# Attention over images on one core: the first query step beside the last key tiles, and the next pair's first convolution early among the queries

## What is computed

```python
x = x + conv_block(group_norm(x))      # 1x3, 5x5 and 1x5 convolutions, a correlation over 7 shifts
t = to_tokens(x)
t = t + attention(layer_norm(t))       # the change lies here
t = t + experts(layer_norm(t))         # top-8 tokens for each of 32 experts

def attention(x):                      # 16 heads of 64
    q = elu(x @ wq.T + bq) + 1;  k = elu(x @ wk.T + bk) + 1;  v = x @ wv.T + bv
    kv_cos, kv_sin = sum_s (k*cos) v,  sum_s (k*sin) v          # 64 x 64 for each head
    o = (q*cos) @ kv_cos + (q*sin) @ kv_sin
    denom = 1 / ((q*cos) @ sum_s(k*cos) + (q*sin) @ sum_s(k*sin) + 1e-5)
    return (o * denom) @ dense_w.T + dense_b
```

## Time and profile before

| | |
|---|---|
| time, median of 3 runs | 3526.32 us (3520.82 to 3526.87) |
| the profiled execution's own time | 3529.31 us |
| its span, first to last instruction | 3527.5 us |
| mean granted clock of TensorE | 0.982 of full speed |
| PE busy | 3191.5 us, 90% of the span |
| DVE busy | 2415.9 us, 68% |
| ACT busy | 1975.6 us, 56% |
| POOL busy | 1968.3 us, 56% |

### The profile page before, as it was taken

One profiled execution on the slowest core, in us unless ns is written; L12 is line 12 of the kernel. 1 busy time (PEld: TensorE's weight loads), 2 busy tenths in 40 slices (PEclk: granted clock), 3 DMA queues, 4 the chain that ended last, 5 costly groups with the idle time before them and its releaser, 6 DMA issues.

```text
span 3527.5 us, 44913 instructions
## 1 busy us (share of the span) xinstructions
PE 3191.5 (90%) x17092; PEld 1488.6 (42%) x17092; DVE 2415.9 (68%) x2773; ACT 1975.6 (56%) x2209; POOL 1968.3 (56%) x1303
## 2 busy tenths in 40 slices
PE   3898999989899998989989898998989999899977
PEld 2543345434443335433454344443354333543333
DVE  5887766967668676776668666686756866645754
ACT  1166654766556764666646665476645676444430
POOL 1167861878428882478727785297833888121320
PEclk8999999999999999999999999999999999999988
DMA  2002740046300661016510363005620075202678
GB/s 55 19 1 57 156 104 28 1 98 146 82 19 0 145 143 56 1 29 152 133 31 0 80 152 85 28 1 125 141 60 19 2 161 135 52 1 65 149 169 279
DMA packets 69297, 278.75 MB, mean 79 GB/s; under 512 B 30845, under 2 KB 35485, under 8 KB 64221
## 3 DMA queue, kind: packets, MB, share of 16 engines
q1 hardware_dynamic: 69085, 275.89, 32.5%
HBM read 242.78 MB, written 33.05 MB: 78 GB/s over the span
## 4 chain that ended last, share of the span: by engine, by line
PE 72%; DVE 11%; ACT 7%; DMA 5%; issue 4%; SPq 1%; POOL 0%; DVEq 0%; ACTq 0%; POOLq 0%
PE ps_D L1590 15%; PE ps_C L1523 10%; PE ps_A L1508 5%; PE ps_B L1508 5%; PE ps_D L1523 5%; PE ps_E L1568 5%; PE ps_E L1523 5%; PE ps_B L1552 3%; PE ps_D L1366 3%; PE ps_A L1552 3%; DVE region L1149 2%; PE ps_A L1385 2%; DMA RB<-r_keep 2%; DVE arena L1000 2%; DMA r_keep<-RR 2%
## 5 line engine op out<-in xcount | busy, mean ns | idle before, releaser
L610 POOL TENSOR_TENSOR arena<-arena,UHL 128x896 f32<-128x896 f32 x525 | 1106.6, 2112 | 252.8 <-ACT UHL L771 252.6
L1590 PE MATMUL ps_D<-region,small 128*128 128x448 f32 x1792 | 759.3, 550 | 9.7 <-DVE OS L1185 6.6
L592 POOL TENSOR_TENSOR region<-region,RB 128x896 f32<-128x896 f32 x224 | 468.9, 2093 | 174.9 <-DMA RB<-r_keep 174.5
L771 ACT ACTIVATE UHL<-arena,W8C 128x896 f32<-128x896 f32 x525 | 540.9, 1033 | 0.4
L620 POOL TENSOR_TENSOR UA<-region,CS 128x128 f32<-128x128 f32 (+1 forms) x400 | 224.6, 563 | 449.4 <-PE ps_C L1523 401.3
L1590 PEld LDWEIGHTS ps_D<-region,small 128*128 128x128 f32 x1792 | 322.9, 190 | 291.8 <-issue 237.8
L815 ACT ACTIVATE EQ<-ps_B,NEG 128x896 f32<-128x896 f32 x224 | 225.5, 1007 | 361.4 <-PE ps_B L1552 361.4
L1523 PE MATMUL ps_C<-region,UA 128*128 128x512 f32 (+1 forms) x800 | 382.5, 601 | 18.1 <-ACT region L689 18.1
L1000 DVE SCALAR_TENSOR_TENSOR arena<-arena,W8C 128x448 f32<-128x448 f32 (+1 forms) x235 | 358.3, 1545 | 0.0
L1158 DVE TENSOR_TENSOR region<-region,ps_C 128x896 f32<-128x896 f32 x224 | 242.9, 1084 | 142.3 <-ACT ps_C L779 142.0
L1125 DVE SCALAR_TENSOR_TENSOR region<-region,ps_A 128x1024 f32<-128x1024 f32 (+1 forms) x200 | 242.6, 1213 | 140.2 <-ACT region L797 140.2
(11 more groups left out here) (308 smaller groups left out, 4983.8 us busy)
## 6 DMA issues: line engine op xcount, KB each, us to landing
RB<-r_keep SPq DMA_DIRECT2D x448, 448.0 KB, 6.0
arena<-x SPq DMA_DIRECT2D x8, 1568.0 KB, 6.6
t_keep<-Y SPq DMA_DIRECT2D x7, 1568.0 KB, 5.2
r_keep<-RR SPq DMA_DIRECT2D x448, 7.0 KB, 2.9
w_keep<-region SPq DMA_DIRECT2D x7, 784.0 KB, 5.5
arena<-w_keep SPq DMA_DIRECT2D x4, 784.0 KB, 10.6
arena<-L_ffn_weight SPq DMA_DIRECT2D x1, 2080.0 KB
CST<-cst SPq DMA_DIRECT2D x1, 1568.0 KB, 6.4
```

The source lines that it names most:

```text
L592: pool.tensor_tensor(out=q, in0=q, in1=RB[:, cc].rearrange("p (c n) -> p c n", c=2), op=ALU.mult).then_inc(pool_scaled.sem, 1)
L610: pool.tensor_tensor(out=X[:, cut], in0=X[:, cut], in1=PRODUCT[m % 3], op=ALU.add).then_inc(pool_taps.sem, 1)
L771: act.activation(PRODUCT[m % 3].rearrange("p (h w) -> p h w", w=W), g_window(2 * g * ROWS + 2 * (k // 5), 2 * (k % 5) - 4, 2 * ROWS), ACT. ...
L1590: ins = pe.matmul(here.area(key)[:, 0:PIX], MW[i][:, c, :], Q[s % 3][:, c, :], start=c == 0, stop=c == NCHUNK - 1)
```

## The change

Three things move, and no work is removed or added.

1. Step 0 of the queries (first image) moves into the key tiles of the second image: the two head matrices of the first image go behind `k_project` of tiles 29 and 31, the four `q_project` of step 0 behind that of tiles 33, 35, 37 and 39, the denominators to tile 41, the sums and the reciprocal to tile 43. All of these use ps_C, one after the other. DVE's part stands one tile later, and in the eight tiles 30, 32, 34, 36, 38, 40, 42 and 43 DVE does no depthwise piece; six pieces go to tiles 44 to 49, two to slots 12 and 15. Step 0's features lie in buffers that are free at that time, and its chunks 0 and 2 are scaled by DVE out of SBUF (`first_scale`), without ACT's copy to PSUM.
2. The slots begin with step 1 and are 66 in place of 70. The head matrices of the second image stand in slots 1 and 3, the four outputs of step 0 in slots 2, 4, 6 and 8. `q_project(1, 0)` goes ahead of the last `k_products`.
3. The four parts of `front` go from slots 57, 59, 61 and 63, in ps_A and ps_B, to slots 4, 6, 8 and 10, in ps_C. The slots of the tap products become a little denser, four in five slots in place of three in four.

The diff, cut to its core: the constants, the uses of the PSUM areas, then DVE's function and PE's.

```diff
-K_PIECES, FRONT_PIECES, Q_PIECES, DRAIN_PIECES = 1, PIECES, (1, 0, 0, 1), 1
-PRODUCT_TILE, PRODUCT_SLOT, POOL_LAG, DRAIN_SLOT = 20, 3, 4, 64
+FRONT_PIECES, Q_PIECES, DRAIN_PIECES = PIECES, (1, 0, 0, 1), 1
+HEAD_TILES, FIRST_TILES, FIRST_DEN, FIRST_SUM = (29, 31), (33, 35, 37, 39), 41, 43
+NO_PIECE = (30, 32, 34, 36, 38, 40, 42, 43)
+PRODUCT_TILE, PRODUCT_SLOT, POOL_LAG, PIECE_SLOT, DRAIN_SLOT = 20, 1, 1, 12, 60
-PRODUCT_SLOTS = {PRODUCT_SLOT + n + n // 3: n for n in range(POOL_PIECES - TILE_PRODUCTS)}
-SLOTS = 4 * STEPS
+PRODUCT_SLOTS = {PRODUCT_SLOT + n + n // 4: n for n in range(POOL_PIECES - TILE_PRODUCTS)}
+SLOTS = 4 * (STEPS - 1)
+HEAD_SLOTS = (1, 3)
+FIRST_OUT_SLOTS = {2: 0, 4: 1, 6: 2, 8: 3}
+FIRST_POOL_SLOTS, FIRST_PARTS_SLOT = {0: 1, 2: 3}, 10
-FRONT_SLOTS = {SLOTS + s: g for g, s in enumerate((1, 3, 5, 7))}
-ALL_SLOTS = 70
+FRONT_SLOTS = {4: 0, 6: 1, 8: 2, 10: 3}
+ALL_SLOTS = 66
...
-            uses += [(("m", i, g), misc()) for i in range(2) for g in range(2)]
+                uses += [(("m", 0, HEAD_TILES.index(k)), "C")] if k in HEAD_TILES else []
+                uses += [(("qp", 0, FIRST_TILES.index(k)), "C")] if k in FIRST_TILES else []
+                uses += [(("den", 0), "C")] if k == FIRST_DEN else []
+                uses += [(("dsum", 0), "C")] if k == FIRST_SUM else []
...
-                uses += [(("t2", FRONT_SLOTS[j]), "AB"[FRONT_SLOTS[j] % 2])] if j in FRONT_SLOTS and not last else []
+                uses += [(("t2", FRONT_SLOTS[j]), "C")] if j in FRONT_SLOTS and not last else []
...
+            def first_scale(here, cc):
+
+                q = features(0, cc)
+                dve.wait_ge(*spread_loaded[cc // 2].at(here.pair, 1))
+                dve.tensor_tensor(out=q, in0=q, in1=RB[:, cc].rearrange("p (c n) -> p c n", c=2),
+                                  op=ALU.mult).then_inc(first_scaled.sem, 1)
...
+                    if k - 1 in HEAD_TILES:
+                        head_matrices(here, 0, HEAD_TILES.index(k - 1))
+                    if k - 1 in FIRST_TILES:
+                        q_features(here, 0, FIRST_TILES.index(k - 1))
+                    if k == FIRST_DEN + 1:
+                        den_parts(here, 0)
+                    if k == FIRST_SUM:
+                        den_guard(here, 0)
+                        den_reciprocal(here, 0)
+                    if conv and k > NORM_TILE and k not in NO_PIECE:
+                        depthwise(here, pair + 1, 1, DVE_PIECES)
+                first_scale(here, 0)
...
+                    if k in HEAD_TILES:
+                        head_matrices(here, 0, HEAD_TILES.index(k))
+                    if k in FIRST_TILES:
+                        q_project(here, 0, FIRST_TILES.index(k))
+                    if k == FIRST_SUM:
+                        q_sums(here, 0)
+                    if k == KTILES + 1:
+                        q_project(here, 1, 0)
...
+                    if j in HEAD_SLOTS:
+                        head_matrices(here, 1, HEAD_SLOTS.index(j))
...
+                    if j in FIRST_OUT_SLOTS:
+                        q_output(here, 0, FIRST_OUT_SLOTS[j])
```

More of the change, by code:

```diff
@@ L95, in slot_of_step, with step_of, chunk_of @@
 def slot_of_step(j, lag):
[L96 removed]
+    return j >= lag and (j - lag) % 4 == 0 and (j - lag) // 4 < STEPS - 1
+def step_of(j):
+    return j // 4 + 1
+def chunk_of(j):
+    return j // 4 + 1, j % 4
 def copied_slot(j):
@@ L676, in tokens @@
                     act.wait_ge(*square_free)
+                if which == 2 and g == 0:
+                    act.wait_ge(*here.filled(("out", 0)))
                 src = here.area(key)[:, 0:m * P].rearrange("p (t c) -> p t c", c=P)
@@ L789, in products_out, with q_exponential @@
                         .then_inc(*here.empty(key))
+            def q_exponential(here, s, cc):
+                key = ("qp", s, cc)
+                act.wait_ge(*here.filled(key))
+                act.activation(EQ[:, cc % 2], here.area(key)[:, :].rearrange("p (c n) -> p c n", c=2)[:, :, 0:PIX],
+                               ACT.Exp, bias=NEG1[:, 0:1]).then_inc(eq_ready.sem, 1)
             def pair_of_images(here):
@@ L808, in pair_of_images @@
                         products_out(here, 0)
-                products_out(here, 1)
                 for j in range(ALL_SLOTS):
                     if j < SLOTS:
[L813 to L817, removed]
+                        q_exponential(here, *chunk_of(j))
+                    if j == 0:
+                        products_out(here, 1)
                     if here.span == "loop" and j in PRODUCT_SLOTS:
@@ L1145, in q_features @@
                 dve.wait_ge(*eq_ready.at(here.pair, n + 1))
-                if s >= 3:
+                if s == 1 and cc == 0:
+                    dve.wait_ge(*ua_ready.at(here.pair, KTILES))
+                if s >= 4:
                     dve.wait_ge(*(here.filled(("out", s - 3)) if cc == 3
@@ L1587, in q_output @@
                 pe.wait_ge(*(scaled_by_pool(here.pair, s, cc) if cc in POOL_SCALED
-                             else here.emptied(("rb", s, cc))))
+                             else here.emptied(("rb", s, cc)) if s else first_scaled.at(here.pair, cc // 2 + 1)))
                 for c in (2 * cc, 2 * cc + 1):
-                    ins = pe.matmul(here.area(key)[:, 0:PIX], MW[i][:, c, :], Q[s % 3][:, c, :],
+                    ins = pe.matmul(here.area(key)[:, 0:PIX], MW[i][:, c, :], features(s, cc)[:, c % 2, :],
                                     start=c == 0, stop=c == NCHUNK - 1)
@@ L1618, in pair_of_images @@
                         k_products(here, k - 2)
+                    if k == FIRST_DEN:
+                        for g in range(2):
+                            q_denominators(here, 0, g)
                     if k in UTS_TILES:
```

139 lines of the change are left out of this document (77 added, 62 removed).

## The result

The changed kernel takes 3603.97 us (median of 4 runs, 3601.97 to 3607.94) against 3526.6 for the kernel before: a ratio of 1.0219, with a 95% interval from 1.0197 to 1.0241. It is 77 us slower. The sign was forecast, the size was not: 3549 was predicted, with 3571 as the upper end.

The account below looks back on a forecast made before the run. PE was taken as the fullest engine, so its idle time was summed: 3.7 - 2.4 + 0.5 + 1.2 = +3.0 us a loop pair, +21 for seven, +1.3 for the last; together +22 on 3526.3, 3549 us (range 3518 to 3571).

Parts of the forecast that it names:

- Key tiles: Key tiles: 7.15 us of added waits for ps_C less 3.4 us given back by the pieces, net +3.7 a pair.
- Start and steady steps: Start of queries: idle 8.7 against 11.1 us, -2.4; steady steps: two pieces in DVE's queue beside POOL, +0.5 a pair.
- front(0): Start of queries: front's first part waits 1.8 us for ps_C from the copy of head (1,1).
- front(3): Start of queries: front's last part, sharing ps_C with the spread of step 1, waits 2.6 us (0.3 to 3.0).
- the denominators: Start of queries: step 1's denominators wait 2.0 us behind first_scale(2), POOL and a copy.
- a piece until 4.3, POOL's turn until 6.4: Start, counted in us from the end of k_project(49): DVE's piece, then one POOL instruction; PE waits 0.8 at q_project(1,2).
- Tail: Tail of a loop pair: without front as cover, waits of outputs add idle time, +1.2 us (0 to 3.6).
- the last pair: Last pair: key tiles lose 6.0 us, start gains about 4.7, tail keeps its length, +1.3; its tail also served as model.
- D: Rival, slower still: tail gives back 5 of 8.7 us, start gains nothing, +7 a pair, 3576 us; chance 0.10.
- B: Rival, faster: the freed start is filled and keeps about 4.4 us of idle, -1.8 a pair, 3515 us; chance 0.19.
- C: Rival, no change: only the port is kinder, start keeps 5.9 us of idle, +0.2 a pair, 3529 us; chance 0.14.
- the two take turns: Start of queries: DVE and POOL alternate at the port, so first_scale waits at most one POOL instruction of 2.08 us.

Follow-up runs that it names:

- without the longest wait: Changed kernel with only POOL's two scalings of step 0 moved from slots 0 and 2 to slots 3 and 5: 3554.64 us.
- all three edits: Changed kernel with POOL's scalings in slots 3 and 5, step 0's PE work behind k_products in the key tiles, and front back in the tail: 3432.83 us.
- The same four matmul groups early: Kernel before with only the four parts of front moved to slots 4, 6, 8 and 10, in ps_C: 3532.4 us, ratio 1.0008.

## Why the prediction was wrong in size

By its own steps, for a loop pair (mean of seven), +3.0 forecast and +10.5 measured:

- **Key tiles**, +3.7 forecast, +3.6 measured: right. The waits were to be 7.15 and are 5.9 (1.83 at the second head where 2.3 was taken, 0.88 four times where 1.15 and 1.03 were, 0.51 for the sums). Of the 3.4 that the pace of the pieces was to give back, 2.3 came: the rest of a pair is that much shorter. Tiles without a part of step 0 take 2.58 us now, and short gaps at the added steps keep the difference. From start to start, tiles 29 to 49 took 55.14 us and take 66.15; 7.0 of the difference is step 0's own work, by the same operations in the kernel before, which leaves +4.0.
- **Start and steady steps**, -2.4 and +0.5 forecast, together +0.5 measured: the start is the step that failed. The sum of its waits was to be 8.7; the single waits of the timeline make 10.6 (5.54, 1.40, 0.51, 0.51, 2.61). `front(0)` (1.8 forecast), `front(3)` (2.6) and the sums were near; the denominators, given 2.0, did not wait, because PE itself came so late. The terms "a piece until 4.3, POOL's turn until 6.4" were the error. DVE was given the port after one POOL instruction at most, and the piece got it after three: 5.81 us, where 1.7 was taken. DVE also came to that piece about 1.5 us late (the `k_features` ahead of it ends at 2445.88, some 4.1 behind `k_project(49)`, not 2.6). So 0.8 us became 5.54.
- **The clock**, not in the sum at all, +3.6 measured. Idle time was taken to cost its own length. Behind the waits of 5.54 and 2.61 come 1.5 and 1.6 us more, 3.1 a pair. Two more low stretches stand in each pair of the changed kernel, about 10 us behind its beginning and 10 ahead of its end:

```profile
2301.70:2305.10 3.40, 3.40 (x18) 2.01 (x17) 1.82 (x2) 0.81 (x2) 0.40 (x1) 0.52 0.00 0
...
2707.90:2711.30 3.40, 2.77 (x26) 2.80 (x28) 1.98 (x3) 1.37 (x3) 3.40 (x4) 0.52 0.00 0
```

  They cost 3.3. The first comes with a wait of 2.27 for the first key products, which both kernels have in every pair; in the kernel before, five of the seven pairs show the stretch. So that kernel lost 2.9 by the clock on average, against 6.5 now.
- **Tail**, +1.2 forecast, +2.8 measured: mis-sized. Its waits are 6.97 now (0.84, 1.12, 2.25, 1.25, 0.72, 0.79) against 4.16 before (0.84, 1.81, 0.72, 0.79), +2.8. The time from output to last tokens, forecast as 29.5, is 31.17:

```profile
2623.26 3.17 PE L1653 MATMUL ps_D<-region,small 128*128 128x448 f32 x8
...
2644.16 3.27 PE L1653 MATMUL ps_D<-region,small 128*128 128x448 f32 x8 [2.25 <-DVE OS L1235]
...
2654.43 1.30 PE L1482 MATMUL ps_A<-CEN,Y 128*128 128x128 f32 x8 [0.79 <-DVE Y L1243]
```

  The last pair's tail was a poor model, as the text suspected: its longest wait for OS is 1.28, and it has none for the scaled queries. That the tap sums make the difference was not tried.

The errors add up: 2.4 at the start and in the steady steps, 3.6 by the clock, 1.6 in the tail, -0.1 in the key tiles; that is the 7.5 us that are missing. That the last pair came near, +2.6 for +1.3, is luck: its waits fell by 4.5 us, and the clock cost 7.2 more. The rivals failed too. D had the right sign and named the tail, but it was too small as well (3576), with no place for the port or the clock; B and C rested on a kinder port.

The port's rule was the open point, and the prediction said so: the Trainium skill (page "SBUF — State Buffer", section "SBUF: two separate sides") has the two engines block each other for whole instructions. The traces agree: 5.81 us for a piece of 0.68. Who goes next was filled in with "the two take turns" from the pieces in the key tiles. Those all stand beside the pair of a tap sum and a UA product, and there DVE does get in. It was a true reading of one pattern, carried to another.

What stays open: why DVE gets in between a tap sum and a UA product without any such wait on POOL. The run with the two added waits shows what hands the port over, not all that does. Nor does any run show why one wait is followed by a low stretch and another is not: without the longest wait a pair lost 6.6 us by the clock, with it 6.5, and with all three edits 0.6.

## What to carry to other kernels

Where VectorE and GpSimd both work out of SBUF, look at what GpSimd has standing ready in a row: a VectorE instruction can wait for the whole row, so keep long GpSimd instructions apart, or put a wait between them, where VectorE is on the path. When work is moved into another stage through a single buffer, place it at that point of the cycle at which the buffer has just been emptied; here the same matmuls cost 5.9 us ahead of the products and 0.2 behind them. And work moved to fill idle time pays only if that idle time is still there once the other part of the change has taken effect. Where TensorE is the fullest engine, count its waits and the time it works at the lower clock apart: here an edit could mend the one and leave the other as it was.

## What the runs showed that was not expected

- POOL kept the port over three instructions in a row, 6 us, against a waiting DVE; two waits of POOL on its own results, 0.1 us of gap each, ended that and made the kernel 37 us faster.
- In the changed kernel, waits of 5.5 and 2.6 us on PE were each followed by about 4 us of work at a granted clock of 0.56 to 0.58 and cost 1.5 and 1.6 us more than their length. With the long wait gone, the same wait of 2.6 was followed by a longer stretch, 6.8 us at 0.50.
- With all three edits the clock cost 0.6 us a pair in place of 6.5: about a quarter of what they gained over the changed kernel in a loop pair.
- The same four matmul groups early were worth nothing in one kernel (ratio 1.0008) and cost 52 us in the other.
